# Image attention on Trainium2: in half of the slots the second head's scores go first

## What is computed

```python
B, T, _ = h.shape
Wh = (h @ W).reshape(B, T, NUM_HEADS, HEAD_DIM).transpose(0, 2, 1, 3)
scale = 1.0 / HEAD_DIM ** 0.5
scores = jnp.einsum('bhtd,bhsd->bhts', Wh, Wh) * scale
attention = jax.nn.softmax(jax.nn.leaky_relu(scores, negative_slope=NEG_SLOPE), axis=-1)
h_prime = jnp.einsum('bhts,bhsd->bhtd', attention, Wh)
...
t = t + _L2_attn_ref(_ln_t(t), L2_attn_W)
```

## Time and profile before

| | us |
|---|---|
| median of 3 runs | 11489.68 |
| the 3 runs | 11482.52, 11489.68, 11515.75 |
| the profiled execution | 11510.12 |
| its span, first to last instruction | 11508.3 |
| the image attention's stretch in it, first exponential to last update of `t_sb` | 838.5 (6785.2 to 7623.7) |

### The profile page before, as it was taken

One profiled execution on the slowest core, in us unless ns is written; L12 is line 12 of the kernel. 1 busy time (PEld: TensorE's weight loads), 2 busy tenths in 40 slices (PEclk: granted clock), 3 DMA queues, 4 the chain that ended last, 5 costly groups with the idle time before them and its releaser, 6 DMA issues. The chain is left out here.

```text
span 11508.3 us, 84579 instructions
## 1 busy us (share of the span) xinstructions
PE 6869.3 (60%) x21895; PEld 2896.9 (25%) x21895; DVE 7327.9 (64%) x5584; ACT 4837.5 (42%) x5351; POOL 7215.9 (63%) x4635
## 2 busy tenths in 40 slices
PE   0178888888888888888878979950000010000569
PEld 0133333333333333333333323320000000000432
DVE  8689999999999999999992257741111111112334
ACT  0066666666666666666652236631111111110123
POOL 0078888888888888888873220017777777775037
PEclk8599999999999999999997679975555555555569
DMA  0145555555555555555551000012222222220022
GB/s 9 31 134 155 152 157 154 156 156 154 156 153 156 153 156 154 157 155 154 156 147 24 1 10 1 1 5 37 18 18 18 18 20 18 18 18 8 3 53 89
DMA packets 388258, 959.55 MB, mean 83 GB/s; under 512 B 124306, under 2 KB 159762, under 8 KB 385762
## 3 DMA queue, kind: packets, MB, share of 16 engines
q1 hardware_dynamic: 303106, 930.59, 29.2%
q0 software_dynamic: 75808, 26.27, 5.2%
q10 hardware_dynamic: 9216, 1.05, 0.1%
HBM read 905.24 MB, written 50.92 MB: 83 GB/s over the span
## 5 line engine op out<-in xcount | busy, mean ns | idle before, releaser
L502 POOL TENSOR_TENSOR hC<-h,Cb 128x1024 f32<-128x1024 f32 x1536 | 3610.4, 2359 | 936.5 <-DVE h L581 935.0
L581 DVE TENSOR_TENSOR_SCAN h<-dA,B_ps 128x1024 f32<-128x1024 f32 x1536 | 3512.4, 2287 | 68.1
L285 PE MATMUL y_ps<-hC,con 128*128 128x512 f32 x6144 | 2909.8, 595 | 92.5 <-DVE gz L587 56.9
L432 ACT ACTIVATE dA<-delta,negA 128x1024 f32<-128x1024 f32 x1536 | 1762.5, 1148 | 1835.6 <-DVE h L581 1835.0
L2514 POOL DMA_INDIRECT g_got<-scratch_node,g_idx x2048 | 1946.1, 950 | 614.4 <-issue 614.2
L573 DVE TENSOR_TENSOR B_ps<-dx,B_ps 128x1024 f32<-128x1024 f32 x1536 | 1856.3, 1208 | 93.2 <-PE B_ps L279 93.2
L2530 PE MATMUL g_ps_y<-g_wout,g_hid 128*128 128x64 f32 x512 | 126.2, 428 | 2248.4 <-ACT g_hid L2570 2248.4
L285 PEld LDWEIGHTS y_ps<-hC,con 128*128 128x128 f32 x6144 | 1136.9, 189 | 1127.3 <-issue 740.5
L279 PE MATMUL B_ps<-Bpart,sel 96*128 96x512 bf16 x3072 | 925.7, 383 | 676.0 <-DVE h L581 674.9
L2600 DVE TENSOR_TENSOR g_e<-g_tgt,g_got 128x128 f32<-128x128 f32 x64 | 27.1, 423 | 1759.9 <-DMA g_got<-scratch_node,g_idx 1759.9
L2554 ACT ACTIVATE g_w_ps<-g_w 128x128 f32<-128x128 f32 x64 | 18.0, 281 | 1941.2 <-DVE g_r L2615 1941.2
(11 more groups left out here) (470 smaller groups left out, 10158.7 us busy)
## 6 DMA issues: line engine op xcount, KB each, us to landing
Cb<-scratch_c_rows SPq DMA_DIRECT2D x3072, 256.0 KB, 3.9
g_got<-scratch_node,g_idx POOLq DMA_INDIRECT x2048
eb_share<-scratch_gate_rows SPq DMA_DIRECT2D x128, 256.0 KB, 3.4
scratch_edge<-g_out SPq DMA_DIRECT2D x64, 384.0 KB
par<-in_ssm SPq DMA_DIRECT2D x48, 395.5 KB, 5.0
scratch_c_rows<-Crow SPq DMA_DIRECT2D x96, 128.0 KB, 3.7
scratch_place<-s_zero SPq DMA_DIRECT2D x4, 1024.0 KB, 10.4
g_tgt<-scratch_place SPq DMA_DIRECT2D x1, 4096.0 KB, 20.8
```

The source lines that it names most:

```text
L285: last = nc.tensor.matmul(y_ps[:, hs], con[:, K_ID:K_ID + P], hC[k % DEEP][:, hs], start=(k == 0), stop=(k == STEPS - 1))
L432: A(dA[k % DEEP][:, :], delta[d][:, :], ACT.Exp, scale=negA[:, n:n + 1]).then_inc(decay_ready, 1)
L502: G.tensor_tensor(hC[k % DEEP][:, :], hst[k % DEEP][:, :], Cb[k % DEEP][:, :], ALU.mult).then_inc(prod_ready, 1)
L581: V.tensor_tensor_scan(hst[k % DEEP][:, ::step], dA[k % DEEP][:, ::step], B_ps[k % 2][:, ::step], 0.0, ALU.mult, ALU.add).then_inc(scanned, 1)
```

## The change

A function `order(g)` gives the order of the two heads in slot g: (1, 0) where the maxima block of slot g - 1 is one of the first eight, else (0, 1). TensorE issues the two heads' scores in that order, and ScalarE reads them in that order. The semaphore `exped` counts exponentials, not heads, so TensorE's wait now looks up at which place head h stood in the preceding slot.

```diff
@@ -1157,6 +1157,11 @@
         r, odd = divmod(g - 3, 2)
         return r if not odd and 0 <= r < ALL // 2 else None
 
+    def order(g):
+
+        block = maxima_at(g - 1)
+        return (1, 0) if block and block[1] < PER else (0, 1)
+
     slots = range(START, STOP)
...
-                    for h in range(2):
+                    for h in order(g):
                         if g:
-                            pe.wait_ge(exped, 2 * (g - 1) + h + 1)
+                            pe.wait_ge(exped, 2 * (g - 1) + order(g - 1).index(h) + 1)
                         for branch in range(2):
...
                 def exps(g):
-                    for h in range(2):
-                        act.wait_ge(scored, 2 * g + h + 1)
+                    for n, h in enumerate(order(g)):
+                        act.wait_ge(scored, 2 * g + n + 1)
                         if g >= 2:
                             act.wait_ge(maxed, g - 1)
```

## The result

| | before | changed |
|---|---|---|
| median, us (20 runs each) | 11506.63 | 11482.58 |
| lowest and highest | 11482.52 to 11520.66 | 11454.82 to 11498.17 |
| profiled span | 11508.3 | 11464.8 |
| image attention, first exponential's start to last one's end | 830.3 | 799.7 |

The ratio is 0.998 with a 95% interval of 0.9973 to 0.9986: the change saves 0.2%, 16 to 31 us, which is clear of no change but smaller than 0.3%. The rest lies in stages that the change doesn't touch, most of it in the convolution before the attention (8.2 us); no other stage moved by more than 10 us.

A forecast was written before the change was run, and what follows sets the result against it. Image attention was taken as bound by a loop through several engines, none of them full. The terms -30.5 + 0 - 1.6 = -32.1 us took 11489.68 to 11457.6 us (68%), whole range 11436 to 11488.

The forecast's parts named there:

- (1): Odd slots 15, 1 and 3: scores run beside the preceding maxima, 0.71 us at 43 places, -30.5 us.
- (2): Head order turns from slot 4 to slot 5, 15 times: hidden by other waits, 0 us, ends +1.7 and -1.2.
- The slower case: Turns at slots 5 and 13 not covered, 0.92 us each, and more clock drops: +40 us, 11530; 3%.
- (3): TensorE's clock at the standstill before `turn0`: one fall fewer, -1.6 us, ends -8.2 and +1.6.
- The clock rival: TensorE's clock stays up where it fell, at `turn0` and in the last slots: -46.5 us, 11443; 15%.
- the first two rivals: The program-order rival (11482, 5%) and the rival of the wait on VectorE (11474, 9%).
- The program-order rival: TensorE passes start in program order, so only 0.17 us remain at each of 43 places: 7 us, 11482; 5%.
- The rival of the wait on VectorE: VectorE gates the turned odd slots too, so half of (1) is left: -15 us, 11474; 9%.

The follow-up runs named there:

- the changed kernel with the clock held: Changed kernel plus extra maxima products before `turn0` in passes 2 to 12 and in even slots from pass 14's slot 14: median 11458.28 us, ratio 0.9948.
- the reverse order: Against the changed kernel, each slot begins with the head whose strips the preceding maxima use: ratio 1.0045 to the kernel before, stage 887.2 us.
- the filled kernel: Changed kernel with the slot's maxima products issued two extra times before `turn0`, in TensorE's standstill: median 11455.41 us, ratio 0.9961, stage 796.4 us.

## Why the prediction was right and wrong

The forecast of 11457.6 us missed the measured 11482.58 by 25 us. 17 of them come from the base that the saving was taken off, 8 from the saving.

- **(1), 0.71 us at 43 places, 30.5 us: right.** Slots 15 and 1 went from 3.62 to 2.91 us, slot 3 from 5.55 to 4.84, and the exponentials start 1.24 us behind the maxima. Between first exponentials slots 3 to 5 together keep their length but for 0.06 us (10.83 to 10.77), as the lead won there is given back at the turn; TensorE's maxima show the gain.
- **(2), the turn, 0 with ends of 1.7 and -1.2: right, at the gain's end.** The 0.15 us that the odd passes could win is there: -2.28 is three times 0.71 and 0.15. (Of the eight passes that the prediction calls odd, seven are; the eighth is pass 14, which has no `turn0` either.) With the clock held up, (1) and (2) together measured 31.9 us, against 30.5. The slower case had no part of it.
- **(3), one fall fewer, -1.6 us: wrong, in sign and size.** This is the term of the saving that was mis-sized. The profile of the changed kernel has one fall more and two long ones at `turn0`, 13.1 us in place of 7.7: +5.4. Its last pass gave 3.2 back (6.0 to 2.8), so that the clock took 2.2 us in this pair of profiles. Over both pairs the falls took 5 us more after the change, 21 against 16. I had read one profile of before and taken its five falls of 1.6 us as the kind and nearly the most there could be; the second profile shows 13.7 us for the same kernel. The end "one more, +1.6" was too near, as a fall could cost 3.2 and even 4.6 us, a case that the rows of before did not hold. That shorter passes shift the standstill against the clock is not shown either way, since two profiles of one kernel differ as much; the direction was a guess.
- **The clock rival (15%)** was wrong as a forecast for the change, but the changed kernel with the clock held shows what it named: its -46.5 us would take the stage from 830.3 to 783.8, and it measured 785.8. It took extra work to get there.
- **The base: wrong by 17 us, the largest error.** The saving was carried to 11489.68, the median of three runs. The median of 20 runs of the same kernel is 11506.63. With it my -32.1 would have read 11474.5, against 11482.58 measured. I had set the profiled run, 11510.12, aside as 20 us above the median, when it was an ordinary run; and I put a run's scatter at 8 us from the two lowest of three runs, where 20 runs cover 38 us.
- **The sum**: 24 us measured (16 to 31), 32.1 forecast. The first pair of profiles has 30.6 in the stage, the mean of the two pairs 27. As far as the profiles show it, the falls' 5 us are the larger part of the missing 8; two profiles of each kernel don't make that a rule. Where the rest went stays open: it is within the interval of the measurement, and the scatter of the convolution lies on top.
- **The whole range**, 11436 to 11488, does hold 11482.58, but by luck: its upper end was put there for the first two rivals, and neither came.
- **The program-order rival (5%)** would have left 0.17 us a place; the row at 7136.84 against 7136.82 excludes it. What the prediction adds on ends, that no exponential began before both heads' records were through, holds for slot 2 in the earlier trace rows but not in the earlier trace rows: there the exponential began at 7172.41, and the second head's last products started at 7172.57. What the rows bear out is that the first head's exponential does not begin before the first head's own products are through, even where the other head's are.
- **The rival of the wait on VectorE (9%)** would have left half of (1). The slots that (1) counts gained 0.71 in full, so it is out.
- Of the other marks named beforehand these came out: ScalarE's wait down by some 30 (39), an odd pass 2.1 us shorter (2.28), 3.2 us from slot 4's first exponential to slot 5's (3.16), the stretch at 806 us (806.1), and no other stage moved by 10 us. Falls in four of six `turn0` stretches did not: it was six.

## What to carry to other kernels

When small matmuls are packed by row strips, look at which strips two neighbours in the stream share, and not only at dependences, and let the reader take first the result whose strips are free: here that was worth 0.71 us in each loop of 6.1. Measure such a change with the clock held up by extra work in both kernels, for the falls differed by 5 to 11 us between two profiles of one kernel, up to a third of what the change gives. And where the saving is a few tenths of a per cent, base the forecast on the spread of many runs; three are too few.

## What the runs showed of the hardware

- TensorE's clock can fall after a standstill is over: in pass 6 of the changed kernel `turn0` ran at the upper level, 1.09 us, and the sums and `turn1` behind it at the lower, 1.93 and 1.97 us. A fall then cost 3.2 us in place of 1.6.
- It can also fall without such a standstill. In pass 3 with head 1 always first (granted clock 0.57 from 6963 to 6979 us) and in pass 7 of the reverse order (0.57 from 7174 to 7178 us) TensorE had not been idle for longer than 0.47 us, by modelled ends, in the 13 us and more before. What brought these falls on stays open.
- Four extra products of 32 rows are cheaper than a fall: two extra issues of a slot's maxima lengthened pass 2 of the kernel before, which had no fall, by 0.17 us (54.45 to 54.62), and passes with a fall went from some 56.0 us to the same 54.62.
- A wait on DMA that was hidden came through now and then: slot 0's scores wait for the rows that SyncE copies after slot 13. In the filled kernel's pass 9 slot 15 took 4.37 us and not 2.91, with this entry in the list of waits of 7260 to 7275 us (waiting engine, line, releaser, then us and times):

```profile
PEld g_ab L1245 <- DMA g_query<-scratch_m_rows: 1.2, 1, 1.2
```

It stood in one or two passes of four of the seven profiles with the new order in slots 13 to 15, and in none of the five in which slots 15 and 1 kept their 3.62 us, nor in that of the kernel with head 1 always first. That fits shorter slots bringing it nearer, but it was not tried by itself.
